# The rotary step reads query and key from the matmul's PSUM bank instead of from a copy in SBUF

## What is computed

```
def apply_rope(x, pos_ids):
    ang = pos_ids[:, :, None] * inv_freq              # 16 frequencies
    cos, sin = both halves of cos(ang), sin(ang)
    x1, x2 = (x[..., :16], x[..., 16:])
    return x * cos + concatenate([-x2, x1]) * sin

h = ada_rms(x, time_emb, ln1_w, ln1_tw)
q, k, v = h @ Wq.T, h @ Wk.T, h @ Wv.T                # 256, 32 and 32 columns
q, k = apply_rope(q), apply_rope(k)
attn = softmax(q @ k.T / sqrt(32));  ctx = attn @ v   # one k and v for 8 heads
x = x + ctx @ Wo.T
x = x + (silu(h2 @ Wg.T) * (h2 @ Wu.T)) @ Wd.T        # h2: a second ada_rms
```

## Time and profile before

| | us |
|---|---|
| three runs: median (lowest to highest) | 309.8 (308.78 to 311.77) |
| the profiled execution, whole | 313.7 |
| its span, first to last instruction | 311.6 |
| PE busy | 291.3 (93%) |
| DVE busy | 215.4 (69%) |
| ACT busy | 205.5 (66%) |
| POOL busy | 153.9 (49%) |

### The profile page before, as it was taken

One profiled execution on the slowest core, in us unless ns is written; L12 is line 12 of the kernel. 1 busy time (PEld: TensorE's weight loads), 2 busy tenths in 40 slices (PEclk: granted clock), 3 DMA queues, 4 the chain that ended last, 5 costly groups with the idle time before them and its releaser, 6 DMA issues.

```text
span 311.6 us, 7095 instructions
## 1 busy us (share of the span) xinstructions
PE 291.3 (93%) x2412; PEld 244.5 (78%) x2412; DVE 215.4 (69%) x527; ACT 205.5 (66%) x698; POOL 153.9 (49%) x289
## 2 busy tenths in 40 slices
PE   7999979898879989978999999999999999999996
PEld 7879767666757768865987787899888988888985
DVE  4884599979496999988859787576445875463431
ACT  3574399999975998987889865737772342662210
POOL 3658687385976955797424456521424321222000
PEclk9795899999986999999999999999999999999999
DMA  6999532002010010000002000000000000000000
GB/s 185 243 299 331 150 104 97 8 1 70 0 36 0 16 54 3 1 3 0 2 0 69 1 3 0 2 2 17 18 3 2 0 8 28 1 2 25 12 2 34
DMA packets 14035, 14.28 MB, mean 46 GB/s; under 512 B 1568, under 2 KB 12960, under 8 KB 14000
## 3 DMA queue, kind: packets, MB, share of 16 engines
q1 hardware_dynamic: 14000, 13.83, 14.7%
HBM read 12.76 MB, written 1.06 MB: 44 GB/s over the span
## 4 chain that ended last, share of the span: by engine, by line
PE 56%; DVE 19%; POOL 12%; issue 6%; ACT 4%; DMA 1%; SPq 1%; DVEq 0%; POOLq 0%
PE ps_shared L1570 16%; PE ps_shared L1377 8%; PE ps_shared L1379 7%; PE ps_shared L1378 7%; PE ps_shared L1543 4%; DVE z L1265 3%; PE ps_output L1524 2%; PE ps_shared L1508 2%; ACT z L990 2%; PE ps_scores L1497 2%; DVE neg_max L1276 2%; PE ps_scores L1407 2%; PE ps_shared L1413 2%; DMA X<-in_x 1%; PE ps_shared L1397 1%
## 5 line engine op out<-in xcount | busy, mean ns | idle before, releaser
L990 ACT ACTIVATE z<-z,neg_max 128x128 f32<-128x128 f32 x128 | 49.9, 404 | 5.8 <-DVE neg_max L1276 5.8
L830 POOL TENSOR_TENSOR h_lo<-xn,h_hi 128x256 fp32r<-128x256 f32 x32 | 24.1, 756 | 35.5 <-ACT h_hi L954 31.6
L1570 PE MATMUL ps_shared<-Wfc2T,g_h 128*128 128x256 f32 x128 | 33.0, 403 | 0.5 <-DVE g_h L1335 0.5
L1508 PE MATMUL ps_shared<-ident,z 128*128 128x128 f32 x192 | 29.4, 276 | 4.1 <-ACT z L990 1.9
L994 ACT ACTIVATE z<-ps_scores,neg_max 128x128 f32<-128x128 f32 x64 | 22.6, 368 | 14.7 <-DVE neg_max L1282 14.4
L1010 ACT ACTIVATE probsT<-ps_shared 128x512 f32<-128x512 f32 x48 | 28.8, 599 | 4.6 <-PE ps_shared L1508 3.6
L884 POOL TENSOR_TENSOR z<-z,row_inv 128x512 f32<-128x512 f32 x16 | 16.6, 1040 | 28.7 <-DVE row_inv L1290 28.5
L1570 PE MATMUL ps_shared<-WdT,g_h 128*128 128x256 f32 x128 | 30.1, 381 | 0.5 <-DVE g_h L1348 0.5
L1046 ACT ACTIVATE g_a<-ps_shared 128x256 f32<-128x256 f32 x32 | 12.4, 386 | 25.8 <-PE ps_shared L1379 21.4
L1508 PEld LDWEIGHTS ps_shared<-ident,z 128*128 128x128 f32 x192 | 22.0, 140 | 8.7 <-issue 6.3
L1570 PEld LDWEIGHTS ps_shared<-Wfc2T,g_h 128*128 128x128 f32 x128 | 24.2, 199 | 5.0 <-issue 1.0
(11 more groups left out here) (164 smaller groups left out, 884.7 us busy)
## 6 DMA issues: line engine op xcount, KB each, us to landing
gamma<-gamma_scratch SPq DMA_DIRECT2D x8, 256.0 KB, 3.6
stage<-in_Wada SPq DMA_DIRECT2D x6, 256.0 KB, 4.9
X<-in_x SPq DMA_DIRECT2D x4, 256.0 KB, 3.8
stage<-in_Wqkv SPq DMA_DIRECT2D x4, 256.0 KB, 5.5
Wfc2T<-in_Wfc SPq DMA_DIRECT2D x1, 1024.0 KB, 8.1
stage<-in_Wfc SPq DMA_DIRECT2D x4, 256.0 KB, 5.2
WdT<-in_Wd SPq DMA_DIRECT2D x1, 1024.0 KB, 6.7
stage<-in_Wg SPq DMA_DIRECT2D x4, 256.0 KB, 2.6
```

What stands on the lines that cost most here:

```text
L830: pool.tensor_tensor(h_lo[:, m, :, j * P:(j + 1) * P], h_full[:, m, j, :, :], h_hi[:, m, :, j * P:(j + 1) * P].bitcast(F32), ALU.subtract) ...
L990: ins = act.activation(z[:, d, u, :], z[:, d, u, :], ACT.Exp, bias=neg_max[:, d, u:u + 1], accum_out=head_sum[:, n % 2, t, u, b:b + 1])
L1508: ins = pe.transpose(bank[:, u * P:(u + 1) * P], z[:, G % DEEP, u, :], ident[:, :])
L1570: ins = pe.matmul(psum[b][:, 0:C], g_h[:, f, j * P:(j + 1) * P], WT1[name][:, f, :], start=(f == 0), stop=(f == FT - 1))
```

## The change

Four functions change; the planner's steps, their lengths, the lists and `PLAN` are as they were.

- ACT copies only the 32 value columns, to a new tile `v1`, and raises a new semaphore `v1_copied` instead of the bank's `freed`. Its wait for the rotary step two before is gone, as there is no query and key copy to overwrite.
- DVE's three rotary products read query and key from the PSUM bank. `rope` waits for `v1_copied`. Once its products have ended it raises the bank's `freed` itself, in an instruction of its own between the products and the additions.
- `values` reads `v1`, and its first group of each n now waits for the bank's `freed` in layer 1 too.

```diff
-                o, j = ord1(n), n % 2
+                j = n % 2
                 key = ("qkv1_product", n)
                 act.wait_ge(*is_filled(key))
-                if o >= 2:
-                    act.wait_ge(rope_ready, o - 1)
                 if last_same(n) >= 0:
                     act.wait_ge(*values_done(last_same(n)))
-                act.activation(qkv1[:, j, 0:QKV1], bank_of(key)[:, 0:QKV1], ACT.Copy).then_inc(is_freed(key)[0], 1)
+                act.activation(v1[:, j, :], bank_of(key)[:, C + D1:QKV1], ACT.Copy).then_inc(v1_copied, 1)
...
             def rope(n):
-                o, j, s = ord1(n), n % 2, seq_of(n)
-                dve.wait_ge(*is_freed(("qkv1_product", n)))
+                o, j, s, key = ord1(n), n % 2, seq_of(n), ("qkv1_product", n)
+                dve.wait_ge(v1_copied, o + 1)
...
-                src = qkv1[:, j, 0:C + D1].rearrange("p (h e f) -> p h e f", e=2, f=HALF)
+                turned = bank_of(key)[:, 0:C + D1]
+                src = turned.rearrange("p (h e f) -> p h e f", e=2, f=HALF)
...
-                                  qkv1[:, j, 0:C + D1].rearrange("p (h f) -> p h f", f=HALF), cs, ALU.mult)
+                                  turned.rearrange("p (h f) -> p h f", f=HALF), cs, ALU.mult)
...
                 ins.then_inc(rope_parts, 1)
                 dve.wait_ge(rope_parts, o + 1)
+                dve.sem_inc(is_freed(key)[0], 1)
...
-                if G == first and layer_of(n) == 0:
-                    pe.wait_ge(*is_freed(("v_product", n)))
+                if G == first:
+                    pe.wait_ge(*is_freed(("v_product" if layer_of(n) == 0 else "qkv1_product", n)))
...
-                    stat = v_pad[:, j, h, :] if layer_of(n) == 0 else qkv1[:, j, C + D1:QKV1]
+                    stat = v_pad[:, j, h, :] if layer_of(n) == 0 else v1[:, j, :]
```

More of the change, by code:

```diff
@@ L579, in build @@
         v_pad = sb("v_pad", [P, 2, H0, QUAD])
-        qkv1 = sb("qkv1", [P, 2, QKV1])
+        v1 = sb("v1", [P, 2, D1])
         rope_c = sb("rope_c", [P, 9, 2, HALF])
@@ L624, in build @@
         qk_high, qk_low = sem("qk_high"), sem("qk_low")
+        v1_copied = sem("v1_copied")
         rope_parts, rope_ready = sem("rope_parts"), sem("rope_ready")
```

## The result

The changed kernel takes 312.52 us in the median of 20 runs (311.16 to 314.75), the kernel before 310.74 us in 20 runs beside it. The medians are 1.8 us apart; the ratio over all the runs is 1.0072, with a 95% interval of 1.0050 to 1.0093, so the change costs 2.2 us (1.6 to 2.9). That is slower, but by less than the 1% that was put down as what one can tell, and by about half of the 4.15 us that the sum gave. The profiled execution took 312.2 us with a span of 310.2 us, against 313.7 and 311.6 before. These two single executions can't be set against each other as they stand: before had the half-clock stretch behind 91.63 us, and after has none there, so at 115 us the changed kernel is 4.15 us ahead (by chance the figure of the forecast's sum).

The account below looks back on a forecast made before the run. No one engine bounds the kernel throughout, but PE is full from 187 us on. Terms of +2.35, +0.10, -0.55 and -0.25 make +1.65; with +2.5 for the clock, +4.15 on 309.8 gives 314.0 us, range 312.2 to 315.9.

Parts of the forecast that it names:

- the rival without a fall: PE stands still at n = 11 but the granted clock stays full: +1.65 us, 311.5 us, chance 0.32.
- The standstill at n = 11: PE's `probs_turn` of group 35 waits about 2.5 us for the bank until DVE's sine products end: +2.35 us net.
- n = 6 and n = 10: PE's wait for the banks of these two rotary steps: nothing at the first, +0.1 us at the second.
- n = 7: DVE's rotary products there are no longer held up by POOL: -0.55 us, bounds 0 and -1.46.
- n = 14: PE's wait for the end of this rotary step shrinks by half: -0.25 us, bounds 0 and -0.49.
- The products in PSUM: Reading PSUM costs DVE nothing, bounds -0.01 and +0.01 us for each of the 24 rotary products.
- The copy: ACT's copy of 32 columns takes about 177 ns; the time saved on ACT counts only at n = 14.
- Sum without the clock: All terms over the rotary steps, before any fall of the granted clock: +1.65 us, bounds +0.4 to +2.7.
- The clock: Granted clock falls to half behind PE's standstill at n = 11: +2.5 us, bounds 0 and 3.4.
- The odds of the fall: Behind PE's pause of about 2.5 us a fall is likelier than not; forecast case with it, chance 0.52.
- taken up elsewhere: Rival: PE's wait at n = 11 stands where other waits stood; price near nothing, 309.8 us, chance 0.10.
- POOL's hold on DVE: Rival: additions at n = 7 also escape POOL and the standstill goes altogether: 307.9 us, chance 0.06.

Follow-up runs that it names:

- the pause filled: Whole change, plus 9 idle matmul steps in PE's list before `probs_turn` of group 35, against the kernel before: 311.15 us, ratio 1.0046.
- n = 11 alone: The change made only for n = 11, the other seven rotary steps copying as before, against the kernel before: 313.85 us, ratio 1.0102.
- the repeat with n = 11 copied: Second measurement of the change with n = 11 left copying as before, against the kernel before: 308.70 us, ratio 0.9974.
- both cures: Whole change, `probs_turn` of group 35 behind `gate_up`, cosine products written back to PSUM for five n, against the kernel before: 308.45 us, ratio 0.9979.

## Why the prediction was right, and where its sizes were off

The mechanism was right: PE stands still where it was foretold, for as long as foretold, and the clock falls behind it. The number had luck in it. 312.52 us lies 0.3 us inside the forecast's own range (312.2 to 315.9) and just above that of the rival without a fall (310.2 to 312.5). It got there because the kernel before took 310.74 us in the median of 20 runs and not the 309.8 of the three that the forecast was added to. The loss itself, 2.2 us, is nearer to the rival's 1.65 than to 4.15, and it lies within the 1% that had a chance of 0.47 against 0.50 for slower. That the forecast was the right case is seen in the profiles, not in the time.

- **The standstill at n = 11** was forecast at +2.35 us, with 2.4 us to be seen before `probs_turn` of group 35. The trace has 2.40 us, ended by DVE. Right, and it is the one place that costs: leaving out n = 11 ends the loss. The instruction that raises the semaphore cost what was read from the earlier trace rows, 0.15 us between the last product and the addition against 0.14. The wait of 0.17 us at `norm_turn` went away as the sum said, and as much again came back there.
- **n = 6 and n = 10** were put at 0 and +0.10. In after PE has a single wait for a rotary step's bank, the one at n = 11. Right within what can be seen.
- **n = 7** was put at -0.55 and gave -0.69 in the pair of profiles: the step is 0.68 us shorter and PE gets it all by 134.01. The mechanism was as told, down to the last addition held to 0.82 us by POOL.
- **n = 14** was put at -0.25 and gave -0.23 on PE (1.23 to 1.46 in the lead); the wait before `qk1_turn` went from 0.49 us to 0.22. Differences as small as these two aren't told apart by the times.
- **The products in PSUM** cost what they cost in SBUF: 451 ns against 455 in the median. The Trainium skill ("VectorE: DVE Perf Modes", section on the TRN2 errata) has a fixed part of 120 cycles against 58; the trace doesn't agree, and the measurement decides. The copy took 174 to 198 ns, near the 177 worked out.
- **Sum without the clock**: +1.65 forecast, +1.4 (0.9 to 2.0) measured with the pause filled, 1.29 in the pair of profiles.
- **The clock** is the term that was mis-sized: +2.5 forecast, from 2.0 to 3.4 given a fall. The fall came, at the place foretold, but it cost 1.40 us in the profile of after, about 3.0 in that of n = 11 alone, and by the runs 0.8 us, which is not clear of noise. The step that failed was taking the length from the two neighbours on the page, as half-clock work of 4 to 6.77 us, and letting it lose half. After's stretch was 3.41 us long with PE idle in the first 0.17, and at half the clock the six matmuls above lost 0.44 of their time, not half: 3.24 x 0.44 = 1.4. The same share fits the other fall, 6.83 x 0.44 = 3.0. A forecast of one short stretch would have been 1.65 + 1.4 = about 3.1, and 312.9 us. How often the fall is short and how often long was not measured: only the mean clock of each run is there, not its places.
- **The odds of the fall** were drawn from two pauses in one profile, and that was too little. PE has the same pause of 1.5 us before `project` (at 91.66 in the earlier trace rows) in all 14 profiles of this kernel and its versions, and a half-clock stretch stands behind it in three of them: in before, in the repeat with n = 11 copied, and in n = 11 alone. Behind the 2.40 us the fall came in both profiles that have that pause; in the other 12 the clock is full from 176 to 192 us.
- **The rivals.** The standstill without a fall, 311.5 us, is nearly what filling the pause gave. Little was taken up elsewhere: 0.34 us by `norm_turn`, and behind 187 us PE has 0.74 us idle in 115, against 0.37. POOL's hold on DVE, the case for faster, was there with the sizes of the sum, as the additions at n = 7 stayed held.

## What to carry to other kernels

When a copy is taken out so that a slower reader uses the PSUM bank itself, the first thing to look up is who holds the bank next, in the order in which PE issues, and where the reader stands in its own list; here seven of eight places were free and one cost 2.4 us. Such a loss is mended in the order: other PE work ahead of the waiting matmul, or the old copy at that one place, gave back the whole loss. An operand moved from SBUF to PSUM has a worth of its own where another engine holds the reader up, and that worth is found by comparing the shortest with the longest duration of one line. The price of a fall of the clock is best added up from the length of the stretch and the start-to-start times of the same matmuls at either clock, not from half of the stretch.

## What the runs showed of the hardware that was not expected

- A Vector product that reads and writes the same PSUM bank took 465 to 467 ns for 288 columns (five instructions of the kernel with both cures), against 446 to 450 into SBUF: writing back into the bank costs 0.02 us. Groups by line of that kernel:

```profile
L1251 DVE TENSOR_TENSOR ps_shared<-ps_shared,cos_t x5: 465/466/467, 115.4 to 249.1; 128x288 f32<-128x288 f32 x5
L1251 DVE TENSOR_TENSOR rope_c<-ps_shared,cos_t x3: 446/447/450, 111.5 to 179.4; 128x288 f32<-128x288 f32 x3
```

- Of pauses of PE of 2.40 us in after and with n = 11 alone, one was followed by a half-clock stretch that began 0.17 us before PE took up work, the other by one that began 1.34 us after it (181.01 to 182.35), twice as long and twice as dear. The same wait doesn't have one price.
